# The last batch's attention output normalised on VectorE, its weights spread by two hardware queues

## The reference, cut to what matters

```
x = x + 0.5 * ffn0(layernorm(x));  x = x + attn0(layernorm(x));  x = x + 0.5 * ffn0(layernorm(x))
x = x + 0.5 * ffn1(layernorm(x));  x = x + attn1(layernorm(x));  x = x + 0.5 * ffn1(layernorm(x))

attn0: probs = softmax(q k^T / 4);  dropped = probs with key 0 set to 0, divided by its own sum
       out = (0.5 * probs + 0.5 * dropped) @ v, then @ Wo^T + bo
attn1: rope on q and k, causal mask, out = softmax(q k^T / 16) @ v, then @ Wo^T + bo
```

## Time and profile before

| what | value |
|---|---|
| median of 3 runs | 2378.97 us (2378.34 to 2380.49) |
| the profiled execution's own time | 2378.16 us |
| its span, first to last instruction | 2375.1 us |
| first layer's output stage | about 986 to 1049 us |
| second layer's output stage | about 2132 to 2172 us |
| busy in the span: PE, DVE, ACT, POOL | 88%, 70%, 57%, 22% |

### The profile page before, as it was taken

How to read it: one execution, slowest core, us unless ns; L and a number is a source line. 1 busy time by engine, 2 the same in 40 slices (tenths; PEclk the granted TensorE clock), 3 DMA queues, 4 the chain that set the end, 5 groups by cost and what they waited for, 6 DMA issues and landing times. The chain is left out here.

```text
span 2375.1 us, 46350 instructions
## 1 busy us (share of the span) xinstructions
PE 2101.8 (88%) x17859; PEld 1318.5 (56%) x17859; DVE 1670.3 (70%) x2206; ACT 1353.6 (57%) x2612; POOL 530.5 (22%) x583
## 2 busy tenths in 40 slices
PE   4999689999999999859959986639999999987998
PEld 3888433333333333448848875524554555546888
DVE  7776499999999999237754449958777777726433
ACT  3443158888888888414434443314677766661444
POOL 2000321111411411430021105662221212122110
PEclk9999779999999999979979997867999999999999
DMA  4004832434444351210030003354455555311000
GB/s 134 1 0 169 235 52 46 78 62 76 85 82 82 67 94 31 55 36 0 0 113 1 0 0 116 142 136 71 74 100 93 106 94 93 68 48 28 23 22 27
DMA packets 124251, 162.74 MB, mean 69 GB/s; under 512 B 54808, under 2 KB 78104, under 8 KB 124056
## 3 DMA queue, kind: packets, MB, share of 16 engines
q1 hardware_dynamic: 106840, 120.71, 23.7%
q0 software_dynamic: 17216, 39.37, 6.2%
HBM read 95.04 MB, written 63.70 MB: 67 GB/s over the span
## 5 line engine op out<-in xcount | busy, mean ns | idle before, releaser
L1391 DVE TENSOR_REDUCE att_maxes<-att_s_max 128x2 f32<-128x1024 f32 (+2 forms) x832 | 974.0, 1183 | 189.1 <-PE att_s_max L1229 88.7
L1370 ACT ACTIVATE att_probs<-att_s_exp 128x512 f32<-128x512 f32 (+3 forms) x1792 | 888.0, 552 | 242.2 <-PE att_s_exp L1269 118.9
L1293 PE MATMUL att_o_ps<-att_probs,att_v_st 128*32 128x256 f32 (+1 forms) x6912 | 526.3, 376 | 14.9 <-ACT att_o_sb L1349 14.2
L1269 PE MATMUL att_s_exp<-att_q_st,att_k_st 64*128 64x512 f32 (+3 forms) x1792 | 459.7, 475 | 4.2 <-ACT att_probs L1370 3.8
L1229 PE MATMUL att_s_max<-att_k_st,att_q_st 62*128 62x512 f32 (+3 forms) x1792 | 395.5, 418 | 67.3 <-POOL att_k_st L1439 31.2
L1269 PEld LDWEIGHTS att_s_exp<-att_q_st,att_k_st 64*128 64x128 f32 x1792 | 190.0, 184 | 342.6 <-ACT att_probs L1370 295.0
L1293 PEld LDWEIGHTS att_o_ps<-att_probs,att_v_st 128*32 128x32 f32 x6912 | 138.5, 108 | 256.5 <-issue 140.6
L1229 PEld LDWEIGHTS att_s_max<-att_k_st,att_q_st 62*128 62x128 f32 x1792 | 189.5, 194 | 90.6 <-issue 54.8
L1464 POOL TENSOR_TENSOR att_m_parts<-att_m_turned,att_zeros 32x128 fp32r<-32x128 f32 x64 | 28.9, 451 | 524.4 <-ACT att_m_turned L1336 384.1
L584 DVE TENSOR_TENSOR ffn1b_h_lo<-ffn1b_h,ffn1b_h_hi 128x512 fp32r<-128x512 f32 x64 | 44.5, 697 | 111.5 <-PE ffn1b_acc L135 99.7
L1477 POOL DMA_DIRECT2D attention_rows<-att_o_sb x64 | 37.6, 587 | 359.1 <-ACT att_o_sb L1349 359.1
(11 more groups left out here) (297 smaller groups left out, 4113.2 us busy)
## 6 DMA issues: line engine op xcount, KB each, us to landing
att_q_st<-q_parts SPq DMA_DIRECT2D x384, 64.0 KB, 5.5
att_k_st<-k_parts SPq DMA_DIRECT2D x192, 128.0 KB, 5.0
q_parts<-qkv_parts SPq DMA_DIRECT2D x32, 512.0 KB, 3.4
k_parts<-qkv_parts SPq DMA_DIRECT2D x32, 512.0 KB, 2.7
attention_rows<-att_o_sb POOLq DMA_DIRECT2D x64, 256.0 KB, 3.4
output_wide<-attention_weights POOLq DMA_DIRECT2D x48, 256.0 KB, 5.0
v_rows<-qkv_vt SPq DMA_DIRECT2D x16, 512.0 KB, 2.9
att_v_raw<-v_rows SPq DMA_DIRECT2D x32, 256.0 KB, 5.8
```

The source lines that it names most:

```text
L1269: mm = pe.matmul(s_exp[:, plan.bank[place], q0:512], k_st[rows, it.set, pr, kt * P:(kt + 1) * P], q_st[rows, it.set, qc, pr, q0:512], star ...
L1293: mm = pe.matmul(o_ps[j * VW:(j + 1) * VW, cols], v_st[:, it.par, kt, j, :], probs[:, step % 2, j, cols], start=kt == 0 and part == 0, sto ...
L1370: act.activation(probs[:, step % 2, j, q0:512], s_exp[:, plan.bank[place], q0:512], ACT.Exp, scale=1.0 if causal else 0.25).then_inc(s["ex ...
L1391: v.tensor_reduce(maxes[:, qc, :, pairs, qt - 4 * qc, kc], banks, AX.X, ALU.max).then_inc(s["max_done"], 1)
```

## The change

1. `spread_weights` takes the tile to fill and the semaphore to raise. For the batches 0 to 2 it gets what it had before.
2. The other engines drain as before.
3. In the output stage the last batch's spreads are issued by SyncE (first half, into `wide`) and by ScalarE (second half, into the new tile `wide_last`), each with a semaphore of its own.
4. Its products are done by VectorE (`normalise_last`): the first half after VectorE's work on chunk 3, the second half after that on chunk 4. In the first layer the three operations of the second weight become two that multiply and add at once.
5. `invert_totals` stands ahead of VectorE's chunk 0, `invert_shares` after chunk 0.
6. `normalise` of the next block's first chunk moves from after chunk 2 to after chunk 4, `TURN_AT` from 5 to 6.

The core of the diff:

```
-        block = ctx.enter_context(nc.Block())
+        block = ctx.enter_context(nc.Block(no_gpsimd_drain=True))
...
+        wide_last = ctx.enter_context(nc.sbuf_tensor(f"{name}_wide_last", [P, E.kinds, KD, CHUNK], F32))
...
-        TURN_AT = 5
+        TURN_AT = 6
...
+        @block.sync
+        def _(sp):
+            spread_weights(sp, E, LAST, 0, E.wide, E.o_sem["last_in0"])
...
             norm_root(act, E, s["next_var"], s["next_std"], NEXT)
+            spread_weights(act, E, LAST, 1, wide_last, E.o_sem["last_in1"])
             part_hi(act, E, T, 0, 0, s)
...
+            def normalise_last(half):
+                n = E.o_sem
+                wide = (E.wide, wide_last)[half]
+                v.wait_ge(n["o_in"], 16 * KD * B)
+                v.wait_ge(n[f"last_in{half}"], 16 * KD * E.kinds)
+                at = slice(LAST * S + half * CHUNK, LAST * S + (half + 1) * CHUNK)
+                rest = E.o_t[:, :, at]
+                if E.kinds == 1:
+                    v.tensor_tensor(rest, rest, wide[:, 0, :, :], ALU.mult).then_inc(n["normal"], 1)
+                    return
+                v.tensor_tensor(rest, rest, wide[:, 0, :, :], ALU.mult).then_inc(s["scaled"], 1)
+                v.wait_ge(s["scaled"], half + 1)
+                for k in range(KD):
+                    ins = v.scalar_tensor_tensor(out=E.o_t[:, k, at], in0=wide[:, 1, k, :], scalar=E.v_first[:, LAST, k:k + 1],
+                                                 in1=E.o_t[:, k, at], op0=ALU.mult, op1=ALU.add)
+                ins.then_inc(n["normal"], 1)
+
+            invert_totals(v, E, LAST)
             for c in range(CHUNKS):
...
+                if c == 0 and E.kinds == 2:
+                    invert_shares(v, E, LAST)
                 if c == 1:
-                    invert_totals(v, E, LAST)
                     norm_rstd(v, E, s["next_step"], s["next_std"], NEXT, n)
-                if c == 2:
-                    if E.kinds == 2:
-                        invert_shares(v, E, LAST)
+                if c == 3:
+                    normalise_last(0)
+                if c == 4:
+                    normalise_last(1)
                     normalise(v, E, 0, 0, s)
...
             store_weights(p, E, LAST)
-            for half in range(2):
-                spread_weights(p, E, LAST, half)
-                normalise_outputs(p, E, LAST, half)
```

More of the change, by code:

```diff
@@ L985, in alloc_outputs @@
     E.o_sem = semaphores(nc, E, name, "stored0", "stored1", "sums_in", "o_in", "total", "total_inv", "share", "share_inv", "step",
-                         "weights", "weights_out", "wide_in", "first_in", "product", "normal")
+                         "weights", "weights_out", "wide_in", "last_in0", "last_in1", "first_in", "product", "normal")
 def fetch_outputs(p, E, b, last):
@@ L1047, in store_weights, with spread_weights @@
     p.dma_start(E.w_dram[b, 0:E.kinds].rearrange("n h (c t) -> (h c) n t", t=P), E.weights[:, :, :]).then_inc(n["weights_out"], 16)
-def spread_weights(p, E, b, half):
+def spread_weights(p, E, b, half, wide, landed):
     n = E.o_sem
@@ L1056, in spread_weights @@
             heads = E.w_dram[b, kind, k * H // KD:(k + 1) * H // KD, half * CHUNK:(half + 1) * CHUNK]
-            p.dma_start(E.wide[:, kind, k, :], heads.unsqueeze(1).to_broadcast([H // KD, HD, CHUNK])).then_inc(n["wide_in"], 16)
+            p.dma_start(wide[:, kind, k, :], heads.unsqueeze(1).to_broadcast([H // KD, HD, CHUNK])).then_inc(landed, 16)
 def normalise_outputs(p, E, b, half):
@@ L1502, in body @@
                         normalise_outputs(p, E, b, 0)
-                        spread_weights(p, E, b, 1)
+                        spread_weights(p, E, b, 1, E.wide, E.o_sem["wide_in"])
                     store(it, 0)
@@ L1513, in body @@
                     elif it.hg == 2:
-                        spread_weights(p, E, b, 0)
+                        spread_weights(p, E, b, 0, E.wide, E.o_sem["wide_in"])
                     elif it.hg == 3:
@@ L1533, in out_stage @@
         T = ctx.enter_context(nc.psum_tensor(f"{name}_T", [P, KD, CHUNK], F32))
-        s = semaphores(nc, E, name, "turned", "hi_ready", "lo_ready", "out_done", "x_new", "xn_ready", "next_step", "next_var", "next_std")
+        wide_last = ctx.enter_context(nc.sbuf_tensor(f"{name}_wide_last", [P, E.kinds, KD, CHUNK], F32))
+        s = semaphores(nc, E, name, "scaled", "turned", "hi_ready", "lo_ready", "out_done", "x_new", "xn_ready", "next_step", "next_var", "next_std")
         block = ctx.enter_context(nc.Block())
         LAST = B - 1
-        TURN_AT = 5
+        TURN_AT = 6
         @block.tensor
```

## The result

The changed kernel takes **2351.48 us** (median of four runs, 2349.76 to 2352.87), the kernel before on the same chip 2378.75 (2378.34 to 2380.49). The ratio is 0.9884, with a 95% interval of 0.9867 to 0.9901: faster by 1.2%. The time lies inside the range of 2337 to 2355, 8.3 us above the 2343.2 forecast.

A forecast was written before the change was run, and what follows sets the result against it. A serial chain (weights, store, spread, GpSimd's products, TensorE) was taken to bound the output stages, with drains ahead. Gains of 26.6 and 9.2, together 35.8, from 2378.16 give 2342.4; with the median 0.8 higher, 2343.2 us, range 2337 to 2355.

The forecast's parts named there:

- No drain: First layer's stage opening: the sums' loads go out at about 981.6 in place of 986.69, TensorE starts near 980.
- Reciprocals: First layer, VectorE: first reciprocal done 4.25 us after the load, second at 990.95, spreads issued at 994.95, 13.0 us earlier.
- Spreads: First layer: eight spreads on two hardware queues land 8.5 us after issue, at 1003.45.
- Products: Last batch's products on VectorE: 2.6 us a half, against about 8.1 on GpSimd.
- The rest: First layer, VectorE's work from the spreads' landing, products included: 18.5 us, so the stage ends at 1022.0.
- Second layer: Second layer's output stage: ends at 2161.7 to 2163.6, middle 2162.6, a gain of 9.2 us.
- 9 us of room: Second layer: spreads issued from 2135.4 and used at 2146, so neither queue matters there.
- A: Rival: spreads slow on hardware queues, at 144 GB/s; first layer's stage ends 8.1 us later, 2351; chance 0.12.
- B: Rival: the drain's wait moves into GpSimd's next DMA; stages 5.1 and 3 us later, 2351; chance 0.12.
- C: Rival: TensorE bounds both stages, stopping between chunks 5 and 6; 2.5 and about 1.5 us more, 2347; chance 0.09.
- D: Rival: slower, two queues' repeated reads lower the spreads' rate; gain used up at 62 GB/s; chance 0.01.
- E: Rival: little gain, early reciprocal stalls VectorE and its products cost what GpSimd's did, 8.1 a half; 2356; chance 0.03.

The follow-up runs named there:

- e4: The kernel before with only GpSimd's drain at the attention block's end taken off; 2365.73 us against 2375.58.
- e5: The changed kernel with GpSimd's drain at the attention's end put back; 2356.62 us, 0.9910 of the kernel before.
- e1: The changed kernel with partitions reordered so that a spread's outermost dimension is 16 and not 8; 0.9860 of the kernel before.
- e10: The changed kernel with e1's reordered partitions and all spreads on SyncE's queue, first half first; 2341.41 us against 2377.89.
- e8: The changed kernel with the two reciprocals back behind VectorE's chunks 1 and 2; 0.9921 of the kernel before.
- run 250: Not a run's name: in "e1 and e10 run 250 GB/s", run is a verb and 250 GB/s the rate of their spreads.
- e2: The changed kernel with all eight spreads issued on SyncE's queue, first half first; 0.9858 of the kernel before.
- e7: The changed kernel with all spreads on GpSimd's queue and the shares inverted ahead of chunk 0's statistics; 2340.29 us against 2375.58.
- e6: The changed kernel with the last batch's products back on GpSimd in three operations a half; 2352.8 us, 0.9905 of the kernel before.

## Why the prediction was off by 8 us

Point by point, in the first layer, times against the forecast ones:

- **No drain: right.** TensorE at 980.00 (980 forecast), the first load at 982.68 (981.6). Of the 1.1, 0.65 is a later last store and 0.4 its landing (2.92 to the next issue, 2.5 forecast). e4 and e5 give the edit 9.5 us and, without what the spreads varied by, 8.4; the forecast's 5.1 and 3 for it are the 5.05 and 3.4 of e5.
- **Reciprocals: right.** From the load to the first one's end 4.27 (4.25 forecast). The second ends at 991.92 (990.95), the spreads go out 3.92 behind it (3.99), at 995.84 (994.95): only the start's delay is carried on.
- **Spreads: this step failed.** The term was 8.5 us from issue to landing and measured 14.5, **6.0 too little**. The prediction set it by the four spreads on GpSimd's queue and three loads on SyncE's, "nearest to the loads of 128 partitions, which these also are". What counted was not the number of partitions but how the DMA is cut for a hardware queue: eight pieces, eight DMA engines. Those loads have 128 partitions outermost, the spreads 8 heads. With sixteen engines it is 10.6 (e1), so the engines are 3.9 of the 6.0. The other 2.1 are the second half: the forecast gave eight spreads the time that four had taken, and two queues let the halves share the engines; in order, on one queue, the first half takes 7.15 (e10).
- **Products: right.** 2.59 a half (2.6). **The rest: right.** From the landing to the end 18.27 (18.5).

So the stage ends 6.7 later than forecast: 0.9 at the issue, 6.0 for the spreads, less 0.2. **Second layer:** from the store to the end 36.69, forecast 36.0 (2162.6 - 2126.58). The spreads were used without a wait, as forecast, but by luck: the weights' store took 5.9 us to land (2113.72 to 2119.64) where 2.2 was forecast, and the spreads were used 8.6 after their issue, where e8's took 8.2. Of the "9 us of room" some 0.4 was left, so that neither queue matters in this layer held only just. VectorE waited 1.71 for TensorE's chunk 0, whose end lay at the late side of the bounds. Against the profiled executions' own times the miss is 7.4 us (2349.76, forecast 2342.4): 6.0 and 0.7 in the stages, 1.7 outside them, less 0.9 around the span, which is 7.5 with the rounding; the median lies 0.9 further out. That the time is inside the range is not to the credit of the sum: the range reached up to 2355 to take in A and B, and the 0.6 stood on a sum that was 6 us short in one term.

The rivals. **A** had the right size, 8.1 more, by luck. Its reason, slow hardware queues, was wrong: e1 and e10 run 250 GB/s on them. The attention's 144 GB/s come near the 150 of the spreads for another reason: in that stretch (275 to 310 us) the DMA engines were busy at nine tenths, and over half of the packets were under 512 B; the spreads had half of the engines and packets of 2 KB. And by A the spreads would have taken 16.6 us, not 14.5; the 2 us between were made up elsewhere. A had 0.12, because I argued that full rows into all partitions would flow better than the attention's packets. **B** is refuted by e4. **C**: TensorE does stop ahead of chunk 6 and takes 5.28 for 16 matmuls, but VectorE never waits for it there. **D**: two queues together ran at some 150 GB/s, as one did (e2), far above the 62 that would have used up the gain. **E**: products on VectorE cost a third of GpSimd's.

The Trainium skill (DMA: Bandwidth & Descriptors, Why a DMA increments its semaphore by 16 and not by 1) says that a DMA is spread over the largest number of engines up to 16 that divides the outermost size of both of its sides. By that rule a spread of 8 heads gets 8 engines, and reordered 16; the eight and sixteen small packets to a spread agree, and it would have pointed at the step ahead, though not given its time. The fit of a DMA's time that the prediction weighed, 6.8 us, does not carry over to eight spreads: 14.5 on eight engines, 10.6 on sixteen; the page gives it for one DMA issued by GpSimd.

Still open: whether GpSimd's queue deals each spread to all engines or to another eight each time; the rows show only that all are busy. Also why the spreads of the same kernel vary between 14.5 and 16.5 us. With that taken out, the drain is worth 5.1 in the first layer, the products 4.6, the reciprocals 4.2, of 20.7 in all. The second buffer, which lets both halves' spreads go out together, and the moved normalising were not tried alone, so where the other 7 come from is not shown.

**Shorter than the change, by the stages:** e10, 2341.41 against 2377.89 (0.9839, stages 77.78), and e7, 2340.29 against 2375.58 (0.9850, stages 76.88), where the change has 85.6 and 85.9. Their ratios are 0.3% or more below the change's first, 0.9884, but only 0.26% and 0.15% below its second, 0.9865, so the run times alone don't settle it. e7's edit, the shares inverted first, could be added to e10, which was not run.

## What to carry to other kernels

Before you move a DMA to another queue, look at its outermost size on both sides: on a hardware queue 8 gave eight DMA engines and 16 gave sixteen, and the duration measured on GpSimd's queue was no measure of it. When two transfers share the DMA engines and one is needed first, put them on one queue in that order: two queues delayed the first half by some 5 us (14.5 to 9.6) and brought the second no earlier. When a layer has room, ask which edit gave it that room before you count on it for another (e8).

## What the runs showed of the hardware that was not expected

- A spread of 256 KB with 8 outermost was carried by eight of 16 DMA engines (eight small packets each, half of the busy share) at some 150 GB/s in all, whether on one hardware queue or two; with 16 outermost, some 250.
- GpSimd's drain took 4.9 and 6.85 us at the attention's end. It is gone from there but stands at the output block's end too, at line 1531, where it begins at 993.5, just behind the weights' store:

```profile
L1531 POOLq DRAIN  x2: 7145/7787/8429, 993.5 to 2113.7; - x2
```

  There 7.1 and 8.4 us cost nothing, since the last statistics end 35 and 30 us after it begins. What it waits for isn't shown. A DMA just issued does not explain it alone: in the second layer, 7 us behind the last spreads' issue, the same drain took 0.7 us before and 5.3 in e4, and in e6's first layer it took 6.3 though GpSimd had issued no DMA for 34 us.
- The weights' store of 64 KB on GpSimd's queue landed 5.9 us after its issue in the second layer (2113.72 to 2119.64), 2.9 us behind two loads of 512 KB on that queue, which took 7.3 to land; that of 128 KB in the first took 2.35 (993.49 to 995.84), 9.8 us behind them. In e8, where the second layer's store goes out 13 us behind them, it took 1.9.
